# Added bfloat16 products into a spare PSUM bank in the softmax edge pass of a four-layer graph network

## What is computed

```python
Q = jnp.einsum('nd,hed->hne', x, Wq)
K = jnp.einsum('nd,hed->hne', x, Wk)
Qr = Q[:, row]
logits = (Qr * K[:, col]).sum(-1) / scale
alpha = jax.nn.softmax(logits, axis=1)
msg = Qr * alpha[..., None]
agg = jax.vmap(lambda m: jax.ops.segment_sum(m, col, num_segments=n))(msg)
```

## Time and profile before

| | us |
|---|---|
| median of 3 runs | 4364.09 |
| lowest and highest | 4363.95, 4365.29 |
| the profiled execution, its time | 4362.5 |
| the profiled execution, its span | 4360.7 |
| TensorE busy (products), share of the span | 3646.0, 84% |
| GpSimd busy | 2881.8, 66% |
| VectorE busy | 2136.9, 49% |
| ScalarE busy | 1362.1, 31% |
| mean granted clock of TensorE | 0.667 |

### The profile page before, as it was taken

The page is one execution under the profiler, slowest core; times in us unless marked ns, Lnnn a source line. Parts: engine busy times, 40 slices in busy tenths (PEclk is TensorE's granted clock), DMA queues, the critical chain, the costliest instruction groups (busy, mean ns, idle before and its releaser), DMA issues. The chain is left out here.

```text
span 4360.7 us, 76651 instructions
## 1 busy us (share of the span) xinstructions
PE 3646.0 (84%) x20596; PEld 3028.2 (69%) x20597; DVE 2136.9 (49%) x6551; ACT 1362.1 (31%) x1910; POOL 2881.8 (66%) x2980
## 2 busy tenths in 40 slices
PE   3649999777668999999996958888888865999997
PEld 1649999766637888888886846656555643777775
DVE  4874444333455555555554844444444446444442
ACT  2000000000041111111112847666666655444441
POOL 4877777777526777777751047777777764777772
PEclk7555555555575555555556978777777775999998
DMA  4532222222263333333322043333333333111112
GB/s 121 197 116 54 53 53 53 53 53 53 63 208 106 79 80 79 79 78 78 79 68 84 21 127 113 100 104 104 104 99 105 104 82 85 50 50 51 50 51 52
DMA packets 258518, 364.29 MB, mean 84 GB/s; under 512 B 53070, under 2 KB 179461, under 8 KB 258309
## 3 DMA queue, kind: packets, MB, share of 16 engines
q0 software_dynamic: 90624, 185.78, 16.5%
q1 hardware_dynamic: 167689, 176.37, 13.4%
HBM read 319.53 MB, written 42.41 MB: 83 GB/s over the span
## 5 line engine op out<-in xcount | busy, mean ns | idle before, releaser
L839 POOL DMA_INDIRECT m_rows<-table,e_idx x832 | 794.2, 955 | 255.8 <-issue 228.6
L839 POOL DMA_INDIRECT m_more<-table,e_idx x480 | 453.7, 945 | 145.6 <-issue 118.5
L1218 PE MATMUL e_agg<-e_weights,m_ones 128*128 128x32 f32 x1568 | 481.8, 401 | 0.0
L839 POOL DMA_INDIRECT m_hT<-table,e_idx x416 | 394.1, 947 | 125.7 <-issue 107.6
L1218 PEld LDWEIGHTS e_agg<-e_weights,m_ones 128*128 128x128 f32 x1568 | 428.5, 333 | 0.0
L839 POOL DMA_INDIRECT e_rows<-table,e_idx x352 | 342.0, 971 | 105.7 <-issue 103.9
L1217 PE MATMUL e_agg<-e_weights,m_more 128*128 128x16 f32 x1152 | 339.8, 375 | 78.3 <-issue 66.3
L1653 PE MATMUL e_z<-e_edge,e_w 128*128 128x512 f32 x392 | 262.8, 806 | 167.2 <-DVEq L1734 152.2
L805 POOL DMA_INDIRECT m_rows<-table,e_idx x320 | 307.9, 962 | 116.0 <-issue 82.3
L1217 PEld LDWEIGHTS e_agg<-e_weights,m_more 128*128 128x128 f32 x1152 | 311.5, 330 | 104.2 <-issue 104.2
L1542 PE MATMUL e_out<-e_counts,e_nodes 128*128 128x256 bf16 x2964 | 383.6, 280 | 0.0
(11 more groups left out here) (315 smaller groups left out, 7057.3 us busy)
## 6 DMA issues: line engine op xcount, KB each, us to landing
e_edge<-edge_T SPq DMA_DIRECT2D x98, 512.0 KB
lu_place<-lo_dram SPq DMA_DIRECT2D x49, 512.0 KB, 3.8
e_key<-key_dram SPq DMA_DIRECT2D x98, 256.0 KB
m_rows<-table,e_idx POOLq DMA_INDIRECT x1152, 2.5
key_dram<-key_out SPq DMA_DIRECT2D x13, 1024.0 KB, 4.7
table<-m_rows SPq DMA_DIRECT2D x39, 256.0 KB, 2.6
e_rows<-table,e_idx POOLq DMA_INDIRECT x528, 2.6
m_more<-table,e_idx POOLq DMA_INDIRECT x480, 2.5
```

Of the source, the lines that this page charges most:

```text
L839: pool.indirect_dma_start(rows[:, t, :], None, table, bass.IndirectOffsetOnAxis(ap=idx[:, t:t + 1], axis=0)).then_inc(landed[t * len(lande ...
L1218: ins = pe.matmul(to[:, 1:3, cols], m.ones[:], both[:, t, :, :], start=False, stop=(t == C - 1))
```

## The change

A helper `fill` issues one bfloat16 product: 128 columns of a constant tile as weights, and 512 columns of it (256, read twice) as the moving operand, into the eighth PSUM bank, `e_unread`. The constant is the float32 tile of column numbers that masks are made from, read as bfloat16. On the narrow path `fill` is called behind each of the eight products and each of the eight sums of a chunk. The increments of `x_ready` and `agg_ready` stay on the last real instruction. Nothing reads the bank.

```diff
-        max_ps = ps("max")
+        max_ps, unread_ps = ps("max"), ps("unread")
+        numbers = m.iota_f[:].bitcast(BF16)
...
+                    def fill():
+                        pe.matmul(unread_ps[:], numbers[:, 0:P], numbers.unsqueeze(1).to_broadcast([P, 2, 2 * P]), start=True, stop=True)
...
                                 ins = pe.matmul(to[:, q * HEADS * W:(q + 1) * HEADS * W], rows_T[:, t, :],
                                                 key[at.b][:, :, ds(rel[t], W)], start=True, stop=True)
-                            ins.then_inc(x_ready, 1)
+                                if q == G - 1:
+                                    ins.then_inc(x_ready, 1)
+                                if not wide:
+                                    fill()
...
                                 ins = pe.matmul(to[:, :, ds(rel[t], W)], s.rows[at.r][:, t, :],
                                                 part[:, q * HEADS * W:(q + 1) * HEADS * W], start=False, stop=(t == C - 1))
+                                if t == C - 1:
+                                    ins.then_inc(s.agg_ready, 1)
+                                if not wide:
+                                    fill()
                             if g < per - 1:
                                 ins.then_inc(weights_read, 1)
-                        ins.then_inc(s.agg_ready, 1)
```

## The result

The median went from 4364.66 (5 runs, 4363.95 to 4366.35) to 4387.78 us (5 runs, 4381.88 to 4388.71). The ratio is 1.0053, with a 95% interval of 1.0039 to 1.0066: 23 us slower. The profiled execution has a span of 4386.0 us, 25.3 more than before. In the trace the loss lies in the softmax edge pass and its end. The next stage's first products (`o_heads_ps`) start 24.3 us later than before, those of the fourth layer (`e_count`) 24.9.

The account below looks back on a forecast made before the run. A 10.02 us loop of VectorE and TensorE, the latter at half clock, was taken to bound the softmax edge pass. 97 x (10.23 - 9.99) = 23 us, plus 5 us at the start, gave 4393 us; range 4346 to 4441.

Parts of the forecast that it names:

- The price of a pair: On TensorE, one real and one added product together take 0.38 us at 2.4 GHz, between 0.32 and 0.50.
- The loop at 2.4 GHz: Softmax edge pass: sums, maximum, its reading and the next build take 9.48 us a chunk, about 9.55 in the mean.
- The wait of 0.87 us every fourth chunk: In every fourth chunk VectorE takes 0.87 instead of 0.41 us before its logits, making that chunk 9.71 us.
- The clock: TensorE's clock in the softmax edge pass rises to 2.4 GHz, then falls again behind the gap before the sums.
- The gap before the sums: TensorE's missing 1.9 us of a 9.55 us chunk, nearly in one piece, while it waits for the weights.
- that sign: A granted clock of 0.8 to 0.9 over the softmax edge pass instead of 0.51 would show the forecast right.
- The price and the number of falls: Each fall of TensorE's clock costs 1.7 us on the sums, in 2 of 5 chunks: mean chunk 10.23 us.
- The beat: Clock turns have their own beat, two falls 10.2 us apart, which holds the mean chunk at about 10.2 us.
- Start and end: The pass starts at 1.2 GHz, so the first chunk's products and first sums add 5 us; no end term.
- GpSimd's 17 us: GpSimd's gathers, 9.98 us a chunk, let the softmax edge pass gain at most 17.5 us, taken as 17.
- the first rival: The clock stays up, chunks of 9.55 us use up GpSimd's lead: 4364 - 17 = 4347 us; chance 0.20.

Follow-up runs that it names:

- gap6_seven: gap6 with the gather of every chunk's eighth tile left out in the softmax edge pass from the eleventh chunk on: 4335.4 us, 0.9936 of the kernel before.
- gap6: The changed kernel with six more added products between the clear and the wait for the weights: 4354.9 us, 0.9977 of the kernel before.
- half_gap6: The changed kernel with 256 columns per added product and six more such products between clear and wait for weights: 4371.0 us, 1.0008 of the kernel before.
- gap_only8: The kernel before with eight added products of 512 columns only between the clear and the wait for the weights: 4371.8 us, 1.0011 of the kernel before.
- half: The changed kernel with 256 instead of 512 columns in each of the sixteen added products: 4387.6 us, 1.0050 of the kernel before.
- prods_only: The changed kernel without the added products behind the sums, those behind the products kept: 4374.1 us, 1.0033 of the kernel before.

## Why the prediction was right

The time forecast was 4393 us, 29 over the median; measured are 4387.8, 23 over. The mechanism is the one forecast: the clock rises, it falls behind the gap in about a third of the chunks, and these falls cost more than the faster sums gain. That the time came within 6 us is in part luck: the loop was taken too short and the falls too dear and too many, which nearly cancel, and the 5 us put at the start are wrong where 3.4 us at the end were left out. Point by point:

- *The price of a pair.* 0.38 us was taken between 0.32 and 0.50. The starts are 0.38 apart at 2.4 GHz and 0.75 at 1.2 GHz (0.76 was taken). So the float32 weight load goes under the added product's columns. The rule of the Trainium skill ("TensorE: Matmul & The Clock Gate", Part 3, what overlaps) that a load runs beside a product only in other row groups does not hold here: by it the prediction made the pair 0.50. That working left out the first pass's own 0.053 us, which would also stand bare, so its bound was too low. The 0.38 us measured are under either.
- *The loop at 2.4 GHz.* 9.48 us for three chunks of four and 9.71 for the fourth were expected, 9.55 in the mean. The 63 chunks without a fall have a median of 9.54 and a mean of 9.66; gap6_seven, almost free of falls, 9.63. The 9.48 was right as a sum, by two errors that cancel: a plain chunk is 0.83 + 3.17 + 0.31 + 5.15 = 9.46, the sums longer than 3.04, and the maximum read after 0.31 and not 0.41. The row that gave 0.41 starts at 1752.58, just behind the fall at 1752.5. The mean was 0.1 us too small, for a delay that was left out. In 26 of the 63 chunks VectorE takes 5.4 us or more from reading the maximum to the next build: in the chunk from 1612.97 line 2009 takes 0.51 us in place of 0.27 (shown above) and line 2016 0.45 in place of 0.28, and the chunk is 9.83 us although VectorE waited only 0.41 us before its logits. What lengthens these instructions was not tried. The wait of 0.87 us every fourth chunk adds little over the 9.71 expected: 9.73 in the three chunks that have it alone.
- *The clock.* It rose within the first chunk, and it fell behind the gap. The gap before the sums was expected at 1.9 us; the waits shown are 1.43 and 1.78 us, with the clear and its issue before them. gap6 shows that the falls need it: with it filled, they went from 34 to 1. half_gap6 and gap_only8, which put work into it too and still have about 50 falls, show that the gap is not all. The mean clock of 0.94 is above the 0.8 to 0.9 that was named as a sign; the prediction's own falls, 3.4 us at half clock in 2 of 5 chunks, make 0.93, so that sign was misworked.
- *The price and the number of falls.* 1.7 us for each in 2 of 5 chunks were expected; measured are 11.21 - 9.66 = 1.55 us in 34 of 97, 0.35 of them. The sums themselves, 4.83 in place of 3.17, are 1.66 us longer. 0.4 x 1.7 = 0.68 a chunk was a little too much, 0.35 x 1.55 = 0.54 is what it is; with the loop of 9.66 in place of 9.55 the two errors nearly cancel: 10.205 against 10.23.
- *The beat.* That a chunk of 9.55 us is held near 10.2 by falls was argued from two falls in another stage, whose chunk is itself 10.06 us long there (2901.29 to 2911.35), so these rows alone could not tell a beat from a chunk. The distances of the falls in the changed kernel, 32 of 33 a multiple of 10.24 us, show it. half and prods_only bear out that it holds the mean in a way that a fixed share of falls would not: with undisturbed chunks of 9.2 to 9.4 us they come to 10.22 and 10.15, and prods_only walks four chunks in 40.94 us again and again. half_gap6, at 10.03 with 50 falls, shows that it does not always hold.
- *Start and end.* 5 us were added for a start at 1.2 GHz. That was wrong in sign: the clock rises so early that the first two builds are 10.27 us apart, where they were 11.91. What was left out instead is the end, where the last sums with their added products are done at 1.2 GHz, 2.2 us.
- *GpSimd's 17 us.* gap6 shortens the pass by 16.3 us, its later chunks waiting for gathers; gap6_seven goes on beyond. So the first rival had its price right for a clock that stays up. The rule of the Trainium skill named beside it ("TensorE: Matmul & The Clock Gate", "Why this matters for your kernels"), that only longer idle gaps drop the clock, does not agree with falls behind waits of 1.4 to 1.8 us.

## What to carry to other kernels

In this kernel work added to lift TensorE's clock paid only where the clock was then held through the longest gap of the loop, so try it where the engine would wait, not only beside the real products: two products in the gap turned 23 us lost into 10 won. It takes both: the gap filled without the others (gap_only8) cost 5 us. Before doing so, look for the next bound: here the gathers leave 17 us in the pass and no more. And when the clock falls in a part of the chunks, look at the distances between the falls: in three kernels here faster chunks brought more falls and no time.

## What was not expected of the hardware

- prods_only keeps a step of 10.24 us a chunk (40.92 to 41.02 us for four, from the 30th chunk on), though a chunk without a fall can be 9.2 us; half has 10.24 in the mean over the same chunks, with four chunks between 39 and 43 us, and the changed kernel has 10.20. The number of falls differs: 48, 73 and 34.
- A real product costs less behind an added one than behind another real one. Its two passes take 0.16 us (1614.28 to 1614.44 above), where bare passes start 0.112 us apart at 2.4 GHz (the median in the filter pass of the kernel before, line 1675), 0.22 for two. An added product of 0.213 us thus lengthens the sums by only 0.16 us for each tile at 2.4 GHz.
